# Decoder layer on one core: the keys of a head group divided as 122, 122 and 64 instead of 103, 103 and 102, with the 64s of two groups turned together

## What is computed

```
q, k, v = split_heads(x @ W_q + b_q), split_heads(ctx @ W_k + b_k), split_heads(ctx @ W_v + b_v)
scores = einsum('bhqd,bhkd->bhqk', q, k) / sqrt(32)
scores = where(mask == 0, -1e6, scores)
attn = softmax(scores)                                   # 16 heads x 77 keys for each token
out = einsum('bhqk,bhkd->bhqd', attn, v)                  # the product "weigh_values"
x = layernorm(x + out @ W_o + b_o)
x = layernorm(x + x @ dequantized(kernel) + bias + (x @ a) @ b)
```

## Time and profile before

| | |
|---|---|
| three executions | 965.21, 968.82, 971.74 us; median 968.82 us |
| span of the profiled execution | 964.6 us (its first to its last instruction; what lies around it is not in the profile: the three times are 0.6 to 7.1 us above it, the median 4.2 us) |
| mean granted clock of TensorE | 0.982 |
| busy: PE, PEld | 917.6 us (95%), 754.5 us (78%) |
| busy: DVE, ACT, POOL | 666.7 us (69%), 376.8 us (39%), 337.8 us (35%) |
| chain of work that ended last | PE 41%, DVE 4%, ACT 2%, POOL 2% |

### The profile page before, as it was taken

How to read it: one execution, slowest core, us unless ns; L and a number is a source line. 1 busy time by engine, 2 the same in 40 slices (tenths; PEclk the granted TensorE clock), 3 DMA queues, 4 the chain that set the end, 5 groups by cost and what they waited for, 6 DMA issues and landing times.

```text
span 964.6 us, 14638 instructions
## 1 busy us (share of the span) xinstructions
PE 917.6 (95%) x4476; PEld 754.5 (78%) x4476; DVE 666.7 (69%) x1128; ACT 376.8 (39%) x1403; POOL 337.8 (35%) x310
## 2 busy tenths in 40 slices
PE   5898999999999999999779999999999999999987
PEld 4784888888888888888668788888888888888775
DVE  3363466665656565555667888979889798887957
ACT  3152120101010111102287566656567565666610
POOL 2000243232222232324236434444443444433733
PEclk9998999999999999999979999999999999999999
DMA  5944201221203020203423122131222203120021
GB/s 179 326 148 172 90 1 52 80 80 52 104 28 127 3 87 1 88 23 116 134 81 102 25 79 73 40 113 24 89 63 78 75 21 122 30 89 21 17 77 44
DMA packets 72346, 76.02 MB, mean 79 GB/s; under 512 B 38567, under 2 KB 40871, under 8 KB 72303
## 3 DMA queue, kind: packets, MB, share of 16 engines
q1 hardware_dynamic: 72303, 75.49, 24.4%
HBM read 52.60 MB, written 22.87 MB: 78 GB/s over the span
## 4 chain that ended last, share of the span: by engine, by line
PE 41%; DVE 4%; ACT 2%; issue 2%; POOL 2%; POOLq 0%; DVEq 0%
PE shared_ps L74 31%; PE score_ps L74 4%; PE shared_ps L1146 4%; ACT probs L1352 2%; PE shared_ps L1109 1%; PE shared_ps L1179 1%; POOL probs L1501 1%; DVE score_ps L1658 1%; DVE xT_lo L1615 0%; DVE x_and_res L1704 0%; DVE top_s L1663 0%; DVE pT_lo L1642 0%; POOL x_and_res L1516 0%; DVE y L1682 0%; DVE w_o_lo L1825 0%
## 5 line engine op out<-in xcount | busy, mean ns | idle before, releaser
L1352 ACT ACTIVATE probs<-score_ps,top_s 128x77 f32<-128x77 f32 x512 | 159.0, 359 | 36.9 <-DVE top_s L1663 36.9
L1352 ACT ACTIVATION_READ_ACCUMULATOR probs<-score_ps,top_s 128x1 f32 x512 | 122.9, 240 | 0.0
L1501 POOL TENSOR_TENSOR probs<-probs,per_total 128x616 f32<-128x616 f32 x64 | 82.7, 1309 | 65.9 <-DVE per_total L1670 65.7
L1494 POOL TENSOR_TENSOR rstd<-ve,half_power 128x1 f32<-128x1 f32 x64 | 42.4, 662 | 157.1 <-DVE ve L1693 152.5
L722 POOL TENSOR_TENSOR vals<-qs_prod 128x512 f32<-128x512 f32 x32 | 41.1, 1296 | 127.1 <-DVE qs_prod L804 127.1
L713 POOL TENSOR_TENSOR mix_rstd<-mix_ve,half_power 128x1 f32<-128x1 f32 x32 | 22.0, 688 | 175.4 <-DVE mix_ve L823 175.4
L1658 DVE COPY_PREDICATED score_ps<-hidden,masked 128x616 f32<-128x616 int32 x64 | 66.2, 1034 | 11.6 <-PE score_ps L74 11.6
L1359 ACT ACTIVATE pT_hi<-shared_ps 103x512 fp32r<-103x512 f32 (+1 forms) x96 | 54.7, 612 | 46.0 <-PE shared_ps L1146 45.5
L672 ACT ACTIVATE v_sb<-v_ps 128x512 f32<-128x512 f32 x32 | 18.9, 594 | 133.9 <-PE v_ps L74 133.9
L679 ACT ACTIVATE qT_hi<-vals 128x512 fp32r<-128x512 f32 x32 | 19.4, 631 | 122.3 <-POOL vals L722 106.2
L1642 DVE TENSOR_TENSOR pT_lo<-shared_ps,pT_hi 103x512 fp32r<-103x512 f32 (+1 forms) x96 | 64.5, 684 | 0.0
(11 more groups left out here) (218 smaller groups left out, 2660.1 us busy)
## 6 DMA issues: line engine op xcount, KB each, us to landing
x_tok<-in_x SPq DMA_DIRECT2D x8, 1024.0 KB, 5.9
x_res<-in_x SPq DMA_DIRECT2D x8, 1024.0 KB, 8.0
x_between<-mix_x SPq DMA_DIRECT2D x32, 256.0 KB, 2.0
x<-x_between SPq DMA_DIRECT2D x8, 1024.0 KB, 5.5
x_tok<-x_between SPq DMA_DIRECT2D x8, 1024.0 KB, 5.7
out<-y_out SPq DMA_DIRECT2D x32, 256.0 KB, 2.0
wqkv_sb<-in_w_qkv SPq DMA_DIRECT2D x4, 768.0 KB, 7.8
keys_split<-w_q_hi SPq DMA_DIRECT2D x8, 154.0 KB, 5.4
```

The lines of the kernel that those rows point to most:

```text
L1352: nc.scalar.activation(probs[:, t % 2, j * KEYS:(j + 1) * KEYS], score_ps[:, g, k * KEYS:(k + 1) * KEYS], ACT.Exp, bias=top[:, t % 2, j:j ...
L1494: nc.gpsimd.tensor_tensor(rstd[:, n:n + 1], ve[:, n:n + 1], half_power[:], ALU.pow).then_inc(rstd_ready, 1)
L1501: nc.gpsimd.tensor_tensor(p, p, per_total[:, t % 2, h * heads:(h + 1) * heads].unsqueeze(2) .to_broadcast([P, heads, KEYS]), ALU.mult).the ...
```

## The change

The 308 keys of a group are divided as 122 + 122 + 64. In even groups (0 and 2) the 64 are the last ones, in odd groups (1 and 3) the first ones, so that the 64 of an even group and those of the next odd group lie side by side in `probs` and are transposed by one instruction of 128. The uses P{t}0 and P{t}1 now hold groups 0, 1 and groups 2, 3, each with both chunks of 122; P{t}2 holds the two pairs of 64. That makes 4 + 4 + 2 = 10 transposes a tile.

The new tile `pT_tail` holds for each group 128 rows: its 64 keys' high part and, in the other half of the partitions, their low part. `v_tail_hi` has the values' high part in both halves, `v_tail_lo` the low part in the half where the probabilities' high part is, zero in the other. Two products of 128 rows then give what three of 102 gave: 6 + 2 = 8 a group.

For that, ACT and DVE handle P{t}2 in two instructions each, of 64 partitions and 256 elements. DVE's write from one half of the partitions into the other. Both count up `tail_lo`; DVE waits for that and then counts up `freed` itself. The values take 26 DMAs a sequence, each for two groups, where 12 for four groups were.

```diff
-KC = [(0, 103), (103, 103), (206, 102)]
+TAIL = 64
+CHUNK = (GK - TAIL) // 2
+MAIN = [[0, CHUNK], [TAIL, TAIL + CHUNK]]
...
 def v_pieces():
-    for j in range(GH):
-        for c, (at, size) in enumerate(KC):
-            a, b = max(j * KEYS, at), min((j + 1) * KEYS, at + size)
-            if a < b:
-                yield j, c, a - at, a - j * KEYS, b - a
+    for odd in range(2):
+        for j in range(GH):
+            for c, at in enumerate(MAIN[odd]):
+                a, b = max(j * KEYS, at), min((j + 1) * KEYS, at + CHUNK)
+                if a < b:
+                    yield odd, j, c, a - at, a - j * KEYS, b - a
...
+        def turned_tail(s, t, odd):
+            rows, others = (slice(64 * k, 64 * (k + 1)) for k in (odd, 1 - odd))
+            return (shared_ps[s.bank(f"P{t}2")][rows, 0:2 * P].rearrange("p (g n) -> p g n", g=2),
+                    [pT_tail[r, odd:GROUPS:2, t * P:(t + 1) * P] for r in (rows, others)])
...
             def load_values(i):
+                for odd, j, key in ((0, GH - 1, KEYS - TAIL), (1, 0, 0)):
+                    for part, half in ((0, 0), (0, 1), (1, odd)):
+                        sp.dma_start(v_tail[part][64 * half:64 * (half + 1), odd:GROUPS:2, j * XHD:(j + 1) * XHD].bitcast(F32),
+                                     src[part][bass.ds(i * KEYS + key, TAIL)][:, odd:GROUPS:2, j, :]).then_inc(v_loaded, 16)
...
             def turn_probs(i, s, t, c):
+                else:
+                    for k in range(2):
+                        at = (2 * k + 1) * GK - TAIL
+                        last = nc.tensor.transpose(shared_ps[s.bank(use)][:, k * P:(k + 1) * P],
+                                                   probs[:, t % 2, at:at + 2 * TAIL], ident[:])
...
             def weigh_values(i, s, g):
-                    pe.wait_ge(turned_hi, nth(i, NT * 3, NT * 3 - 1))
+                    pe.wait_ge(turned_hi, nth(i, NT * 4, NT * 4 - 1))
...
+                nc.tensor.matmul(out, v_tail[0][:, g, :], pT_tail[:, g, :], start=False, stop=False)
+                nc.tensor.matmul(out, v_tail[1][:, g, :], pT_tail[:, g, :], start=False, stop=True).then_inc(filled, 1)
...
             def split_probs(i, s, t, c):          # DVE
+                else:
+                    dve.wait_ge(turned_hi, nth(i, NT * 4, 4 * t + 3))
+                    psum, (hi, lo) = turned_tail(s, t, 0)
+                    nc.vector.tensor_tensor(lo, psum, hi.bitcast(F32), ALU.subtract).then_inc(tail_lo, 1)
+                    psum, (hi, lo) = turned_tail(s, t, 1)
+                    nc.vector.tensor_tensor(lo, psum, hi.bitcast(F32), ALU.subtract).then_inc(tail_lo, 1)
+                    dve.wait_ge(tail_lo, nth(i, NT * 2, 2 * t + 1))
+                    dve.sem_inc(freed, 1)
```

More of the change, by code:

```diff
@@ L1017, in x2T_of, with turned_main @@
             return x2T_odd if isinstance(i, int) and i == B and t % 2 else x2T
-        def turned_bank(s, t, c):
-            return shared_ps[s.bank(f"P{t}{c}")][0:KC[c][1], :].rearrange("p (g n) -> p g n", g=GROUPS)
+        def turned_main(s, t, pair):
+            return (shared_ps[s.bank(f"P{t}{pair}")][0:CHUNK, :].rearrange("p (c g n) -> p c g n", c=2, g=2),
+                    [q[:, :, 2 * pair:2 * pair + 2, t * P:(t + 1) * P] for q in pT])
+        def turned_tail(s, t, odd):
+            rows, others = (slice(64 * k, 64 * (k + 1)) for k in (odd, 1 - odd))
+            return (shared_ps[s.bank(f"P{t}2")][rows, 0:2 * P].rearrange("p (g n) -> p g n", g=2),
+                    [pT_tail[r, odd:GROUPS:2, t * P:(t + 1) * P] for r in (rows, others)])
         @block.sync
@@ L1068, in _ @@
                 sp.dma_start(raw, src.rearrange("(c p) n -> p c n", p=P)).then_inc(w_loaded[n], 16)
-            sp.wait_ge(values_cleared, 2)
+            sp.wait_ge(values_cleared, 4)
             for n in range(2):
@@ L1143, in turn_probs @@
                 wait_reuse(pe, freed, s.reusable(use))
-                at, size = KC[c]
-                for g in range(GROUPS):
-                    last = nc.tensor.transpose(shared_ps[s.bank(use)][0:size, g * P:(g + 1) * P],
-                                               probs[:, t % 2, g * GK + at:g * GK + at + size], ident[:])
+                if c < 2:
+                    for k in range(2):
+                        for g in range(2):
+                            at = (2 * c + g) * GK + MAIN[g][k]
+                            last = nc.tensor.transpose(shared_ps[s.bank(use)][0:CHUNK, (2 * k + g) * P:(2 * k + g + 1) * P],
+                                                       probs[:, t % 2, at:at + CHUNK], ident[:])
+                else:
+                    for k in range(2):
+                        at = (2 * k + 1) * GK - TAIL
+                        last = nc.tensor.transpose(shared_ps[s.bank(use)][:, k * P:(k + 1) * P],
+                                                   probs[:, t % 2, at:at + 2 * TAIL], ident[:])
                 last.then_inc(turned, 1)
@@ L1152, in weigh_values @@
                 if g == 0:
-                    pe.wait_ge(v_loaded, nth(i, 1, 0) * (16 * 2 * len(list(v_pieces()))))
+                    pe.wait_ge(v_loaded, nth(i, 1, 0) * (16 * V_LOADS))
                     pe.wait_ge(freed, s.emptied_before("P32"))
-                    pe.wait_ge(turned_hi, nth(i, NT * 3, NT * 3 - 1))
+                    pe.wait_ge(turned_hi, nth(i, NT * 4, NT * 4 - 1))
                 wait_reuse(pe, freed, s.reusable(use))
-                pieces = [([v[0:size, c, g, :] for v in v_block], [p[0:size, c, g, :] for p in pT])
-                          for c, (_, size) in enumerate(KC)]
-                split_matmuls(nc, shared_ps[s.bank(use)][:], pieces).then_inc(filled, 1)
+                out = shared_ps[s.bank(use)][:]
+                terms = [(v_block[a][:, c, g, :], pT[b][:, c, g, :]) for c in range(2) for a, b in ((0, 0), (1, 0), (0, 1))]
+                for n, (l, r) in enumerate(terms):
+                    nc.tensor.matmul(out, l, r, start=(n == 0), stop=False)
+                nc.tensor.matmul(out, v_tail[0][:, g, :], pT_tail[:, g, :], start=False, stop=False)
+                nc.tensor.matmul(out, v_tail[1][:, g, :], pT_tail[:, g, :], start=False, stop=True).then_inc(filled, 1)
             def project_o(i, s, t):
@@ L1357, in split_probs @@
                 act.wait_ge(turned, nth(i, NT * 3, 3 * t + c))
-                size = KC[c][1]
-                nc.scalar.activation(pT[0][0:size, c, :, t * P:(t + 1) * P], turned_bank(s, t, c),
-                                     ACT.Copy).then_inc(turned_hi, 1)
+                if c < 2:
+                    psum, (hi, lo) = turned_main(s, t, c)
+                    nc.scalar.activation(hi, psum, ACT.Copy).then_inc(turned_hi, 1)
+                else:
+                    for odd in range(2):
+                        psum, (hi, lo) = turned_tail(s, t, odd)
+                        nc.scalar.activation(hi, psum, ACT.Copy).then_inc(turned_hi, 1)
             def split_o(i, s, g):
@@ L1543, in step @@
                 root(i, s, "F3")
-            for tile in v_block:
+            for tile in v_block + v_tail:
                 nc.gpsimd.memset(tile[:].bitcast(F32), 0.0).then_inc(values_cleared, 1)
```

26 lines of the change are left out of this document (14 added, 12 removed).

## The result

The changed kernel takes 973.57 us (median of 4 runs, 972.63 to 974.58), the kernel before in the same session 967.13 us (4 runs). The ratio is 1.0066, 95% interval 1.0035 to 1.0097. By the bound of 1% that is no change, but the interval lies wholly above 1: it is a loss of some 6 us, where the forecast had 0.4. The profiled run of after took 972.63 us with a span of 970.8, against 964.6 before: 6.2 us more of span.

A forecast was written before the change was run, and what follows sets the result against it. The prediction took DVE's queue and chain to bound two of three stretches of a loop step, PE one. Steps 1 to 6 +0.6, step 7 +0.6, step 0 0, step 8 -0.8: +0.4 on 968.8, 969 us, range 959 to 976.

The forecast's parts named there:

- the tail on DVE: DVE's low part of P{t}2, one instruction made two plus a wait: 0.40 us more, between estimates of 0.31 and 0.47.
- (a): Loop step from F0 to P12, 12.98 us, paced by DVE's queue: +0.40 us from the tail of P02.
- (b): Loop step from P12 to the end of F3, 18 us, PE alone: -0.41 us from fewer transposes at P12 and P22.
- (c): Loop step from the end of F3 to the next F0, 28 us, a chain: +0.1 us, between 0 and 0.3.
- Steps 1 to 6: The six loop steps, each +0.1 us, together +0.6.
- Step 0: Start of `attend`, without the loop's ring: eight transposes less, four tails more, 0 +- 0.5 us.
- Step 7: Step without query projection, where tails count and transposes don't: +0.6 us, between 0 and 1.2.
- Step 8: V0 to V3 run without a break: four products fewer, -0.92 us, V0 perhaps 0.1 later, taken as -0.8.
- The first, PE as the bound: Rival: PE sets the time, so 13.9 us come off: 955; chance 0.2 for this or more than half of it.
- The third, a tail of 1.0 us: Rival: each half takes as long as a whole, neither overlaps; +0.9 us a step, 976; shares 0.14 with the DMA rival.
- the slower rivals: Two rivals, a DVE tail of 1.0 us (976) and slow DMA issue (974): together 0.14, somewhat over half past 1%.
- the ring's argument: A loop step is three stretches, two of them DVE's; PE's wait grows where its work shrank: +0.1 us a step.

The follow-up runs named there:

- e1: The changed kernel, but DVE's second tail instruction counts up `freed` itself, so DVE no longer waits for its own result; 966.54 us, ratio 1.0004.
- e4: The kernel before, with DVE's low part of P{t}2 divided in two of 256 elements in the same partitions and waited for; 973.99 us, ratio 1.0078.
- e10: e2 with the tail's two transposes issued three times over at P12 and P22, eight more a step; 967.61 us, ratio 1.0015.
- e8: e2 without the last product of the tail in each group, so part of the result is missing; 960.41 us, ratio 0.9945.
- e3: The changed kernel, but POOL starts its split of `w_ffn` only when DVE's split of `w_o` is done; 970.44 us, ratio 1.0032.
- e12: The kernel before with its twelve DMAs of values each divided by groups, 24 in all; 966.75 us, ratio 1.0004.
- e9: e8, but DVE's low part of a tail covers 8 tokens of 128; 959.40 us, ratio 0.9925.
- e2: The changed kernel unstacked: tail halves in tiles of their own, nine products, one ACT and one DVE tail instruction, 24 DMAs; 963.75 us, ratio 0.9964.
- e7: The changed kernel without DVE's wait for `tail_lo` and with POOL's split of `w_ffn` behind DVE's of `w_o`; 965.56 us, ratio 0.9996.
- e6: The kernel before, with only POOL's split of `w_ffn` put behind DVE's split of `w_o`; 966.12 us, ratio 0.9995.
- e11: e2 with the tail's two transposes issued three times over at P02 and P32, eight more a step; 964.62 us, ratio 0.9977.

## Why the prediction was right in class and short in size

**The step that failed is the tail on DVE, taken at 0.40 us "between the two middle values"; it costs 0.85.** Its parts were 0.15 to 0.31 for the two halves and 0.16 for the wait; measured are 0.40 for the halves (e1, with the wait gone) and 0.45 for the wait. That e1's 0.40 is the figure taken for both together is chance. A half takes 0.42 us, as estimated. But the first starts only when `ve` is finished, the second 0.45 behind the first, and the mask 0.45 behind the second (e1); e4's two, in the same partitions, start 0.34 apart. That agrees with the Trainium skill, "VectorE: DVE Perf Modes", section "Two Vector instructions with no wait between them". The wait was mis-sized most: 0.16 us came from a row in which a small instruction waits for statistics; here 0.38 pass behind the end, and the next pair, mask and maximum, is another 0.1 apart. The same page, section "The DRAIN you can't avoid", says that in a chain of copies a semaphore behind each costs nothing extra. Here DVE also waits for it, and the runs say 0.45 us, though the mask does not overlap the half without the wait either (e1: the half ends at 722.74, the mask starts at 722.76); they decide. Why the same kind of wait costs 0.16 in one place and 0.38 in another, no run settles. In after itself, with the same semaphore instruction behind the wait, it is 0.38 ahead of the mask at P02, 0.15 ahead of `qT_lo` at P32 (760.34) and 0.22 ahead of the splits in step 0 (516.90), so the semaphore instruction alone is not it.

**(a) +0.40 against 0.84** follows from that nearly one for one: DVE was the bound of (a), if only by 0.09 us, and its tail's growth reached P12. The wait showed not ahead of P12 but earlier in (a), ahead of O3, 0.47 us.

**(b) -0.41 against -0.37 to -0.40**, right, and e10 gives the same price with the other sign. **(c) +0.1 against 0.0**: inside its range, and no kernel of the table moved it by more than 0.03. The mechanism was right too: the mask behind P32 ends at the same distance from P30 whenever it starts. The products saved there were rightly taken at nothing in a loop step (e8).

**Steps 1 to 6, +0.6**: steps 2 to 6 came to +2.5, 0.47 a step but for the first; step 1 came to -1.5, since a stretch at half clock fell away there.

**Step 0, "0 +- 0.5", was the second failure.** The tail's cost was counted only as a delay. It also moves DVE's split of `w_o` against POOL's of `w_ffn`, and 2.49 us became 5.76. The prediction named such a shift as what would make it wrong, and gave it no place and no price, though both rows stood in the trace of before. e3's profile puts the price at 3.5 us; against before, which had 2.0 of that, it is 1.6 net. Which start is the lucky one stays open: it is not the lead of DVE over POOL alone. With 0.86 us (before) and 0.85 (e12) DVE gets through in 2.5; with 1.15 (e9), 0.90 (e2, e8) and 0.73 (e1) it takes 4.7, with 0.55 and 0.48 (after, e4) 5.8. The Trainium skill, "SBUF — State Buffer", section "Who interferes with whom", has DVE and POOL lock a shared port for an instruction, and the trace agrees: of the four instructions one takes 0.69 us in after and the other three 1.76 to 1.78, in e1 two and two, in before all four 0.69. Rule and rows were used for the mask at 639.98 and not here.

**Step 7, +0.6 (0 to 1.2), measured +3.0**, the largest term of the loss and the third failure, of the same kind as the second: the tail was counted as a delay there too. DVE's mask at 902.51 runs into POOL's addition of 901.96 and takes 1.38 us for 0.87, `y` comes late and F0 waits 1.53. Behind it stands a stretch at half clock from 915 to 919 us, in which PE's products take 1.5 us longer. It is not to be added: e7, without wait and `w_o` collision, has no such stretch and still loses 2.7 us in step 7. In the profiles of before, e6 and e12 the mask is first and takes 0.87 us; in the eleven others POOL is first, the mask takes 1.38 to 1.57, and step 7 loses from 0.3 (e9) and 1.0 (e8) to 4.4 us (e3). e4 is among them with 2.0, so neither the stacking nor the new division is needed for it; a change in DVE's tail is enough. Why a lighter tail (e2, e8, e9) brings the same order stays open. No run takes this meeting out alone, so that it makes the whole of the loss is not shown.

**Step 8, -0.8 against -1.05**, was right: V0 to V3 are four products shorter and nothing later changed. (Against the 10.16 us from V0 to O0 in e12 it is -0.8.)

**The rivals.** The first, PE as the bound, is refuted as stated: e11 has 0.08 or less for eight transposes and e8 nothing for four products. But it holds in (a) as soon as the tail is lighter (e2). The third, a tail of 1.0 us and 976 us, was the nearest in time, not in mechanism: its halves took 0.68 us each where 0.42 were measured, and its step grew by 0.9 where 0.46 were; its point of decision, 0.35, fits e1, where at 0.40 the whole is as long as before. Of the 0.14 given to the slower rivals somewhat over half was put past 1%, but neither 976 nor 974 passes it (978.5), so that share rests on nothing that was worked out.

**How much of the hit was luck.** In the sum's own terms, forecast and measured: steps 0 and 1 +0.1 and +1.75, steps 2 to 6 +0.5 and +2.5, step 7 +0.6 and +3.0, step 8 -0.8 and -1.05, together +0.4 and +6.2. The direction of the ring's argument was right: PE's work fell and its waits rose, and the saving bought nothing. That 6 us stay under 1% of this kernel is a matter of its length, and not of the sum.

## What to carry to other kernels

Read who owns each stretch of a loop's ring before pricing a change: the same eight transposes are worth 0.85 us a step or under 0.1, and a saving on PE that is paid on DVE was worth nothing even when made without a fault. A wait of an engine for its own result is to be priced with what follows it, at the place where it stands, and best removed: here the second instruction could carry the count.

A delay is not only a length. Where it moves an engine against another that shares a port with it, look up each long pair of such instructions and price the unlucky order as a rival. Here two such places, in step 0 and step 7, stand where the profile lost 1.6 us net and 3.0, against 2.5 in the five steps of the loop.
